# Score matmuls over 512 columns, and expert 0's late rows placed by one-hot matmuls instead of through memory

## The reference

```
# 1: causal linear attention: q,k = relu(.)+1e-6; out = (q k^T masked to s<=t) v / row sum
x = layernorm(x + attn(x) @ out_w.T + out_b)
# 2: cross attention, |t-s| <= 64, keys and values are ctx itself
x = layernorm(x + softmax(q k^T / sqrt(8)) @ ctx @ W_proj + b_proj)
# 3: mixture of 8 experts, top 1, capacity int(4096/8*1.25)+1 = 641 rows each
top1 = argmax(softmax(x @ wg)); rank = tokens of the same expert before this one
slot = top1*capacity + rank           # over capacity: dropped
buf.at[slot].set(x); eb = buf.reshape(8, 641, 128)
y = gelu(eb @ W1 + b1) @ W2 + b2      # hidden width 512
x = layernorm(x + where(valid, y[slot], 0) * score)
```

## Time and profile before

| | us |
|---|---|
| median of 3 runs (463.06 to 465.02) | 464.04 |
| the profiled execution, its own time | 465.73 |
| its span, first to last instruction | 464.0 |
| PE busy in the span | 423.5 |
| DVE, ACT, POOL busy | 346.2, 264.5, 257.7 |

### The profile page before, as it was taken

How to read it: one execution, slowest core, us unless ns; L and a number is a source line. 1 busy time by engine, 2 the same in 40 slices (tenths; PEclk the granted TensorE clock), 3 DMA queues, 4 the chain that set the end, 5 groups by cost and what they waited for, 6 DMA issues and landing times.

```text
span 464.0 us, 21013 instructions
## 1 busy us (share of the span) xinstructions
PE 423.5 (91%) x7874; PEld 336.8 (73%) x7874; DVE 346.2 (75%) x1671; ACT 264.5 (57%) x655; POOL 257.7 (56%) x375
## 2 busy tenths in 40 slices
PE   8889999999999999999999999998857999999950
PEld 6666778787878787878787878776637777777650
DVE  4366667788899898899998899787871667777660
ACT  4455667666777666777666777666551344444400
POOL 5433355665566665566665566554662055566673
PEclk9999999999999999999999999999987999999995
DMA  4800000110011110010110010000016034443100
GB/s 133 277 15 16 14 25 15 32 32 28 26 37 27 31 32 27 26 38 27 33 31 27 26 28 15 14 5 26 26 37 202 8 107 116 114 108 90 31 17 20
DMA packets 25719, 22.50 MB, mean 48 GB/s; under 512 B 3606, under 2 KB 21072, under 8 KB 25620
## 3 DMA queue, kind: packets, MB, share of 16 engines
q1 hardware_dynamic: 23284, 16.96, 12.7%
q0 software_dynamic: 2336, 4.20, 2.9%
HBM read 12.13 MB, written 9.58 MB: 47 GB/s over the span
## 4 chain that ended last, share of the span: by engine, by line
PE 82%; issue 5%; DVE 4%; POOL 3%; ACT 2%; DMA 2%; POOLq 0%; DVEq 0%; ACTq 0%; SPq 0%
PE banks L622 24%; PE banks L678 13%; PE banks L958 9%; PE banks L615 7%; PE banks L630 7%; PE banks L940 6%; PE banks L690 3%; PE banks L706 3%; ACT arena L1160 1%; PE banks L656 1%; PE banks L657 1%; PE banks L658 1%; PE banks L758 1%; PE banks L591 1%; DMA expert_in<-x,sidx 1%
## 5 line engine op out<-in xcount | busy, mean ns | idle before, releaser
L1304 DVE TENSOR_REDUCE mx<-banks 128x8 f32<-128x1024 f32 x64 | 77.9, 1218 | 23.4 <-PE banks L630 23.3
L441 POOL TENSOR_TENSOR rs<-ve,minus_half 128x1 f32<-128x1 f32 x32 | 18.2, 569 | 99.6 <-DVE ve L1271 99.2
L678 PE MATMUL banks<-arena,V 128*32 128x128 f32 x2048 | 69.6, 276 | 0.4 <-ACT arena L1019 0.2
L1019 ACT ACTIVATE arena<-banks 128x1024 f32<-128x1024 f32 x64 | 62.2, 1022 | 10.9 <-PE banks L630 10.9
L1160 ACT ACTIVATE arena<-banks,b1T 128x321 f32<-128x321 f32 x64 | 33.8, 528 | 56.1 <-PE banks L940 55.2
L678 PEld LDWEIGHTS banks<-arena,V 128*32 128x32 f32 x2048 | 52.0, 109 | 10.0 <-issue 5.3
L989 ACT ACTIVATE arena<-banks 64x512 f32<-64x512 f32 x60 | 35.3, 588 | 38.7 <-PE banks L630 38.7
L550 POOL DMA_INDIRECT out_x<-ot,idx x40 | 40.4, 1010 | 20.4 <-DVE ot L1704 11.5
L940 PE MATMUL banks<-arena,w_sb 128*128 128x320 f32 (+1 forms) x128 | 38.5, 442 | 3.4 <-DVE r L1679 2.4
L622 PE MATMUL banks<-QE,kT 32*128 32x128 f32 x1024 | 37.5, 282 | 3.3 <-DVE mx L1304 1.3
L472 POOL DMA_INDIRECT expert_in<-x,sidx x32 | 35.1, 1096 | 9.8 <-issue 6.3
(11 more groups left out here) (176 smaller groups left out, 1021.3 us busy)
## 6 DMA issues: line engine op xcount, KB each, us to landing
w_sb<-in_L_ffn_W SPq DMA_DIRECT2D x16, 256.0 KB
expert_in<-zeros SPq DMA_DIRECT2D x10, 266.5 KB, 3.7
EB<-expert_in SPq DMA_DIRECT2D x8, 325.0 KB
X<-in_x SPq DMA_DIRECT2D x32, 64.0 KB, 2.0
C<-in_ctx SPq DMA_DIRECT2D x32, 64.0 KB, 2.5
out_x<-fb SPq DMA_DIRECT2D x32, 64.0 KB
out_x<-ot,idx POOLq DMA_INDIRECT x40
b2b<-in_L_ffn_b SPq DMA_DIRECT2D x1, 512.0 KB
```

Of the source, the lines that this page charges most:

```text
L678: mm = pe.matmul(bank(name)[VW * s:VW * (s + 1), half * P:(half + 1) * P], V[:, h, :], scored[:, h // NA, h % NA, :], start=q == 0, stop=q ...
L1019: nc.scalar.activation(P2[b % 2][:, 2 * half:2 * half + 2].rearrange("p j a t -> p j (a t)"), pair("s2t", half), ACT.Exp, scale=SCALE).the ...
L1304: v.tensor_reduce(mx[b % 2][:, 8 * half:8 * half + 8].rearrange("p (j a) -> p j a", a=NA), pair("s2", half).rearrange("p j (a t) -> p j a ...
```

## The change

Scores of `s1` and `s2` are now made by `by_slot`: four matmuls (eight in the trace), one for each group of rows, each over the 512 columns of its bank. `s2t` keeps `by_head`, since there the weights differ from slot to slot. After the first four mask matmuls a new semaphore (`s1_half`, `s2_half`, `s2t_half`) is raised, and the first half's reader waits for that.

Expert 0's rows reach PSUM in a new way, for that expert alone. SP loads the weights of experts 0 and 1 in the drain, and the rows of expert 0 as they are after batches 0 to 27 into `EB[2]` (`early_rows`); POOL's scatter of batch 28 waits for that load. PE turns them by matmuls that add into banks 4 and 5. For each of batches 28 to 31 a one-hot matrix (128 tokens by 641 slots) is made, for 28 to 30 by two ACT instructions (square, then relu of 1 minus it) and for 31 by two DVE comparisons, and PE multiplies the batch's rows `x2` by it in two halves (`late_rows`). The 28 filler matmuls are gone. DVE copies the two banks to `ebT`, and the first layer of expert 0 waits for that and no longer for `EB[0]`, which is still loaded for the residual and the gate. Expert 1's rows are turned ahead of the last part of expert 0's second layer. On DVE, rk4 moves up behind rk3 of the same batch.

```diff
+            def early_rows():                      # SP
+                for k in range(4):
+                    sp.wait_ge(scattered[k], 16 * (LATE // 4))
+                sp.dma_start(EB[2][:], buf[0:ET * P, :].rearrange("(p c) d -> p c d", c=ET)).then_inc(early_in, 16)
+                sp.dma_start(ER0[:], buf[ET * P:ROWS, :]).then_inc(early_in, 16)
             for n in range(B + LAST + 1):
                 at(load, n + 4)
+                if n == B - 3:
+                    expert_weights(0)
+                    expert_weights(1)
+                if n == LATE + 7:
+                    early_rows()
...
-            expert_weights(0)
-            expert_weights(1)
...
-            for e in range(1, 3):
-                expert_rows(e)
+            expert_rows(1)
+            sp.wait_ge(early_turned, 1)
+            expert_rows(2)
...
+            g.memset(slot_of[:, ET * P:ROWS], float(ET * P))        # POOL, constants
+            g.iota(slot_of[:, 0:ET * P], pattern=[[1, ET], [ET, P]], base=0, channel_multiplier=0,
+                   allow_small_or_imprecise_dtypes=True).then_inc(slots_ready, 1)
...
+                if b == LATE:                                       # POOL, op_scatter
+                    pool.wait_ge(early_in, 32)
...
+            def by_slot(name, weights, moved):
+                for j, used in enumerate(BANKS[name]):
+                    part = slice(VW * j, VW * (j + 1))
+                    pe.matmul(banks[:, used, :], weights[part, :], moved[part, :, :].rearrange("p a t -> p (a t)"),
+                              start=True, stop=False, tile_position=(VW * j, 0))
...
-                by_head("s1", lambda part, a: kT[b % 2][part, :], lambda part, a: QE[b % 2][part, a, :])
-                causal_masks(0)
+                by_slot("s1", kT[b % 2], QE[b % 2])
+                causal_masks(0).then_inc(s1_half, 1)
                 causal_masks(1).then_inc(s1_full, 1)
...
+            def early_rows():                      # PE
+                pe.wait_ge(early_in, 32)
+                for c in range(ET):
+                    for half, (r0, r1) in enumerate(HALVES):
+                        c0, c1 = max(c * P, r0), min((c + 1) * P, r1)
+                        if c0 < c1:
+                            pe.matmul(max_bank[half][:, c0 - r0:c1 - r0], EB[2][:, c, 0:D], ident[:, c0 - c * P:c1 - c * P],
+                                      start=False, stop=False)
...
+            def late_rows(b, half):
+                if b < B - 1:
+                    pe.wait_ge(hot_ready, b - LATE + 1)
+                else:
+                    pe.wait_ge(hot_last, half + 1)
+                r0, r1 = HALVES[half]
+                mm = pe.matmul(max_bank[half][:, 0:r1 - r0], x2[b % 4][:, 0:D], hot[b - LATE][:, r0:r1],
+                               start=(b == LATE), stop=(b == B - 1))
...
-            for _ in range(WARM):
-                pe.matmul(act_bank[0][:, 0:P], ident[:], ident[:], start=True, stop=True)
...
-                act.wait_ge(s1_full, b + 1)
+                act.wait_ge(s1_full if half else s1_half, b + 1)
...
+            def op_hot(b):                         # ACT, batches 28 to 30
+                to = hot[b - LATE]
+                act.wait_ge(slot_ready, b + 1)
+                nc.scalar.activation(to, slot_of[:], ACT.Square, bias=minus_slot[:, b - LATE:b - LATE + 1]).then_inc(hot_square, 1)
+                act.wait_ge(hot_square, b - LATE + 1)
+                nc.scalar.activation(to, to, ACT.Relu, scale=-1.0, bias=ones[:, 0:1]).then_inc(hot_ready, 1)
...
+            def op_hot(half):                      # DVE, batch 31
+                r0, r1 = HALVES[half]
+                v.tensor_scalar(hot[B - 1 - LATE][:, r0:r1], slot_of[:, r0:r1], slot1[:], None, ALU.is_equal).then_inc(hot_last, 1)
...
+                if e == 0:                         # DVE, rows_turned
+                    for half, (r0, r1) in enumerate(HALVES):
+                        dve.wait_ge(t_full, half + 1)
+                        v.tensor_copy(ebT[0][:, r0:r1], max_bank[half][:, 0:r1 - r0]).then_inc(t_done, 1)
+                    return
```

More of the change, by code:

```diff
@@ L218, in decoder @@
         xg, end = late(end, [ET, D])
+        hot = [hT[1][:, k, :] for k in range(B - LATE)]
         act_bank = [banks[:, k, :] for k in range(4)]
@@ L347, in _ @@
                 load(b)
[L349 to L355, removed]
             def expert_weights(e):
@@ L363, in expert_rows @@
                     eb_in[e % 3], 16)
-            expert_weights(0)
-            expert_weights(1)
+            def early_rows():
[3 more added lines that the diff above has]
+                sp.dma_start(ER0[:], buf[ET * P:ROWS, :]).then_inc(early_in, 16)
+            for n in range(B + LAST + 1):
+                at(load, n + 4)
+                if n == B - 3:
[3 more added lines that the diff above has]
+                    early_rows()
+                if n == 0:
+                    clear_rows()
+                    sp.dma_start(b2b[:], b2.unsqueeze(0).broadcast_to([P, E, D])).then_inc(b2_in, 16)
+                    sp.dma_start(b2r[:], b2).then_inc(b2_in, 16)
+                at(fallback, n - 8)
             for k in range(4):
@@ L810, in _, with claim_rows @@
                 at(op_s1, n)
+            def claim_rows():
+                for used in (4, 5):
+                    pe.wait_ge(*last_on[used])
+            def early_rows():
[6 more added lines that the diff above has]
+                                      start=False, stop=False)
+                pe.matmul(max_bank[1][:, ET * P - HALVES[1][0]:ROWS - HALVES[1][0]], ER0[:, 0:D], ident[0:1, 0:1],
+                          start=False, stop=False).then_inc(early_turned, 1)
+            def late_rows(b, half):
[6 more added lines that the diff above has]
+                               start=(b == LATE), stop=(b == B - 1))
+                if b == B - 1:
+                    mm.then_inc(t_full, 1)
             op_y1T(B - 4)
@@ L903, in _ @@
             op_lg(B - 2)
+            claim_rows()
+            late_rows(B - 4, 0)
             op_rk(B - 3)
+            late_rows(B - 4, 1)
             op_rk(B - 2)
@@ L907, in _ @@
             op_lg(B - 1)
+            early_rows()
             op_rk(B - 1)
+            late_rows(B - 3, 0)
+            late_rows(B - 3, 1)
+            late_rows(B - 2, 0)
+            late_rows(B - 1, 0)
+            late_rows(B - 2, 1)
+            late_rows(B - 1, 1)
             pe.wait_ge(slot_ready, B)
@@ L950, in second_layer @@
                 for k in range(JT):
+                    if e == 0 and k == JT - 1:
+                        turn_rows(1)
                     if e > 0 and k < 2:
@@ L1016, in op_p @@
             def op_p(b, half):
-                act.wait_ge(s2t_full, b + 1)
+                act.wait_ge(s2t_full if half else s2t_half, b + 1)
                 wait(act, pv2_full, b - 1)
@@ L1148, in _ @@
             op_x2Te(B - 1)
+            op_hot(B - 3)
             op_fb(B - 2)
             op_lexp(B - 1)
+            op_hot(B - 2)
             op_fb(B - 1)
@@ L1301, in op_mx @@
             def op_mx(b, half):
-                dve.wait_ge(s2_full, b + 1)
+                dve.wait_ge(s2_full if half else s2_half, b + 1)
                 wait(dve, mxs_ready, b - 1)
@@ L1740, in _ @@
                     break
+                if e == 0:
+                    for c in range(2):
+                        summed(e, c, gate_mark)
+                    rows_turned(1)
                 for c in range(ET):
```

54 lines of the change are left out of this document (37 added, 17 removed).

## The result

The kernel after takes 458.27 us (median of 6 runs, 455.39 to 460.63), the kernel before beside it 463.82 (6 runs, 462.88 to 465.02). The ratio is 0.988, 95% interval 0.984 to 0.992: some 5.6 us, or 1.2%, faster. The forecast was 457.2, which was 6.8 us less than the median of 464.04 it started from. The profiled execution of the kernel after has a time of 458.66 and a span of 456.9, against 465.73 and 464.0.

The account below looks back on a forecast made before the run. PE bounds the kernel (82% of the chain), with one large hole of 10.9 us before expert 0's first layer. 465.73 - 2.0 - 0.3 - 4.5 = 458.9; the median stands 1.7 lower: 457.2 us, range 453.5 to 461.5.

Parts of the forecast that it names:

- Long score matmuls: Loop, `s1` and `s2`: 512-column passes save 0.032 us a group, 2.0 us in 64 groups, with full overlap.
- The rival (475): Loop score groups: long streams overlap less, four groups running only as three at a time, + 16 us; chance 0.05.
- Early signals: Half signals come 0.14 us earlier: worth nothing in the loop, 0.3 us in the filling and the drain.
- In the loop PE waits for nobody, so it is worth nothing there: Loop: the 0.14 us earlier half signal gains 0, as PE's waits show almost nothing, 0.7 us at most.
- the half signals matter in the loop: Rival, loop: PE's `s2` loads begin just when ACT ends its first half; up to 4 us more, 453.3; chance 0.10.
- The drain: After the loop: ranks 31 come 2.2 us late, yet expert 0's first layer starts 6.6 us earlier.
- so I let it rise near 350: Drain: PE's clock rises from 1.2 to 2.4 GHz near 350 us, since fillers saw it rise after 3.5 us.
- the clock stays low: Rival: without fillers expert 0's first layer may run at 1.2 GHz, 4.3 us more at most, 461; chance 0.13.
- The way into expert 1: Expert 0 to expert 1's first layer: 5.2 us earlier, 0.7 lost waiting for banks DVE sums, net 4.5.
- the rival of late rows: Before expert 1: its rows land after 363.7, 3 to 5 us more of scatters and loads, 459 to 461; chance 0.10.
- experts farther apart than 10.1 us: Sign of being wrong, expert phase: experts 1 to 7 starting more than 10.1 us apart.
- The experts follow each other at 10.1 us: Kernel before, after expert 0's first layer: PE is filled again, experts 10.1 us apart.

Follow-up runs that it names:

- e1_long: Kernel before with only the long score matmuls of `s1` and `s2`; 458.02 us, ratio 0.996.
- e2_half: Kernel before with only the early half signals (`s1`, `s2`, `s2t`); 457.01 us, ratio 0.993.
- e5_half_dve: Kernel before with only the half signal of `s2` to DVE's maxima; 459.99 us, one run.
- e6_half_act: Kernel before with only the half signals of `s1` and `s2t` to ACT; 464.14 us, one run.
- e3_loop: Kernel before with long score matmuls and half signals, keeping the old way into expert 0; 455.44 us, ratio 0.990.
- c4_order_fill: Kernel after with ranks 31 ahead of the early rows, ACT reordered to match, and 16 fillers in the drain; 454.44 us, ratio 0.979 to kernel before.
- c3_order: Kernel after with ranks 31 ahead of the early rows and ACT reordered to match, no fillers; 458.67 us, ratio 0.988 to kernel before.
- c6_order_fill_turn: `c4_order_fill` with expert 1's rows turned between expert 0's two layers and copied ahead of expert 0's sums; 451.48 us, ratio 0.972 to kernel before.
- c5_fill_turn: Kernel after with 20 drain fillers, expert 1's rows turned between expert 0's layers and copied ahead of its sums; 453.29 us, ratio 0.975 to kernel before.
- e4_expert: Kernel after with short score matmuls and full signals again, so expert 0's part alone; 458.81 us, ratio 0.997 to kernel before.
- c1_changed: Kernel after, unchanged, run again on another chip; 458.45 us, ratio 0.989 to kernel before.

## Why the forecast came out, point by point

**Long score matmuls: right.** 2.0 forecast, 2.1 measured in `e1_long`; a group shorter by 0.032 us in the forecast and in the trace. The overlap of four row groups is full at 512 columns too. The rival (475) is out by `e1_long`. The Trainium skill (TensorE: Matmul & The Clock Gate, section "Measured speedup vs the span model") has 3.07 times for such four tiles; the trace does not agree: at 0.558 us a round the group would have been 0.23 us longer than before, and it was 0.032 shorter.

**Early signals: the step "In the loop PE waits for nobody, so it is worth nothing there" failed.** It rested on the waits of PE, which have next to nothing of a wait that was put down as "issue"; the row of `s1` in the earlier trace rows, with 3.3 us of idle time, was shown and not used. Measured 3.1 us instead of 0.3 (`e2_half`), through DVE's first maximum of `s2` and not through ACT (`e5_half_dve`, `e6_half_act`). The rival "the half signals matter in the loop" was the case, with 3.1 of its up to 4 us, but the place it named, ACT's half, was not the one, and its time of 453.3 did not come. Both parts of the loop gave 4.7 (`e3_loop`) for 2.3.

**The drain: the step "so I let it rise near 350" failed.** PE was busy 8.00 of 8 us from 344 to 352, and the clock stayed at 1.2 GHz until 352.10, past all but the last microsecond of the rows that I had at 2.4 GHz. The twelve passes of late rows behind ranks 31 took 5.63 us; at 2.4 GHz they take 3.75 in `c4_order_fill`.

The terms, from the loop's end. Up to the ranks of 29 the forecast held: batch 30's logits came 1.15 us late (forecast 1.2), these ranks 1.7 (1.7), batch 31's logits 1.8 (1.6). From those logits to ranks 31, with the early rows between, it took 3.78 us instead of 2.5 (343.90 to 347.68, against 348.5 to 351.0), because all fourteen passes of the early rows ran at the low clock; so ranks 31 came 3.6 late instead of 2.2. From these ranks to the first layer it took 5.54 us instead of 3.5 (351.0 to 354.5). Together the first layer came 3.1 nearer to the loop's end instead of 6.6, and both steps of the miss lie in passes that ran at 1.2 GHz. The DVE comparisons took 0.39 instead of 0.45, its copies 0.49 as forecast. That the clock is the cause, `c4_order_fill` against `c3_order` shows: the same work in the same order with fillers, 4.2 us less at the first layer and in the time.

The rival "the clock stays low" had the kind right and the place wrong: the first layer itself ran at 2.4 GHz, the late and early rows before it did not, although they were "real work of the same density".

One term was mis-sized without harm. ACT's wide instructions, in a timeline of ACT of the kernel after, took 0.83 us instead of 0.70:

```profile
337.98 0.83 ACT L1158 ACTIVATE arena<-slot_of,minus_slot 128x641 f32<-128x641 f32 x1 [1.23 <-DVE x L1463]
```

The 0.85 ns a column of the earlier trace rows was from rows that read PSUM, these read and write SBUF; whether that makes the difference was not tried. The first pair started a little earlier than forecast and ended where the forecast had it, 15.0 us from the loop's end.

**The way into expert 1: right in kind and in size.** The forecast had 1.4 us for the turning at the end of expert 0 with DVE's copies behind it (5.2 of 6.6 kept), and 0.7 lost in the first layer, 2.1 together. Measured: the interval from expert 0 to expert 1 is 11.28 for 10.13, 1.15 more, and expert 1's first layer takes 5.27 for 4.33, 0.94 more, 2.1 together. The latter is the wait for DVE's sums: its second, third and fourth pair of passes each start some 0.15 us behind the end of one. The timeline of PE:

```profile
362.66 0.71 PE L990 MATMUL banks<-ident,EB 128*128 128x128 f32 x5
364.50 5.43 PE L1009 MATMUL banks<-arena,w_sb 128*128 128x321 f32 x16
...
375.48 0.71 PE L1009 MATMUL banks<-arena,w_sb 128*128 128x321 f32 x2
376.50 4.25 PE L1009 MATMUL banks<-arena,w_sb 128*128 128x320 f32 x14 [0.32 <-DVE r L1779]
```

Nearly all of it was avoidable: in `c6_order_fill_turn` the two intervals are 10.35 and 10.03. `EB[1]` was not late, so the slack held; the rival of late rows was out here, and came true in `c5_fill_turn`.

**The sum.** Loop 4.7 for 2.3, expert part 1.3 for 4.5: together 6.0, and the change measured 5.6. Each part was mis-sized by more than the whole was off: the right time came of two wrong terms. The prediction's own sign of being wrong, experts farther apart than 10.1 us, appeared: in the kernel after the starts of experts 1 to 7 lie between 10.2 and 11.0 apart. Of these intervals only the first is put down to the change; in `e4_expert`, on the first chip, all the others are 10.03. "The experts follow each other at 10.1 us" was too short for the kernel before as well, where experts 3 to 7 lie 10.9 to 11.0 apart.

## What to carry to other kernels

Before a wait is called worth nothing, look behind "issue": where an engine writes a bank that another has just read, compare the end of that reader with the start of the writer, since the view of waits can leave it out. The same distance in two kernels, here 0.36 us, says that the writer still waits in both. When gaps are filled with real work, read the granted clock of the stretch and cost all of that work at the level it has there, and do not take from one trace when it will rise; matmuls that keep the clock up before the work is due can be worth more than the work moved. When the profiled execution is not the typical one of its runs, say which of the two a number is from. And an own sequence for the first of many rounds should be measured beside the one that the other rounds have.

## What the runs showed of the hardware

The rhythm of the experts depends on the chip. On the first chip all but the first interval of `e1_long` are 10.03 us. On the others, experts 3 to 7 lie up to 11.0 apart, in the kernel before too. The difference is in DVE's sums. In the kernel after, three of them, and in `e4_expert` (first chip) two:

```profile
372.41 0.35 DVE L1779 SCALAR_TENSOR_TENSOR r<-banks,EB,arena 128x128 f32<-128x128 f32 x1 [0.32 <-PE banks L1029]
373.86 0.35 DVE L1779 SCALAR_TENSOR_TENSOR r<-banks,EB,arena 128x128 f32<-128x128 f32 x1 [0.77 <-PE banks L1029]
376.00 0.35 DVE L1779 SCALAR_TENSOR_TENSOR r<-banks,EB,arena 128x128 f32<-128x128 f32 x1 [1.46 <-PE banks L1029]
```

```profile
377.60 0.35 DVE L1779 SCALAR_TENSOR_TENSOR r<-banks,EB,arena 128x128 f32<-128x128 f32 x1 [0.21 <-PE banks L1029]
378.50 0.35 DVE L1779 SCALAR_TENSOR_TENSOR r<-banks,EB,arena 128x128 f32<-128x128 f32 x1 [0.21 <-PE banks L1029]
```

In the latter they follow PE's parts at 0.9 us; in the former they come 1.5 and 2.1 us apart, and the third starts 2 us after PE has ended its part, and the next expert's first layer waits for their banks. GpSimd's indirect DMAs run in that stretch on both chips. What holds DVE back there was not tried and stays open; it is worth 3.9 us in the distance from expert 0's first layer to expert 7's (74.23 us in the kernel before, 70.31 in `e1_long`), about the difference between the chips' times of the kernel before.

A clock that stays at 1.2 GHz for 8 us in which PE has no gap was not expected: in the kernel before, the fillers had run for 3.5 us when it rose. But that was one trace. In the six traces that have the same 28 fillers they ran between 3.3 and 5.9 us until the clock rose, longest in `e2_half`, where they start at 347.23:

```profile
347.30:353.10 5.80, 5.80 (x27) 5.80 (x28) 0.00 (x0) 1.08 (x1) 1.23 (x2) 0.50 0.71 213
353.20:354.00 0.80, 0.80 (x9) 0.80 (x9) 0.00 (x0) 0.00 (x0) 0.00 (x0) 1.00 0.06 17
```

With the early and late rows PE had run without a gap for 6.5 to 8.3 us when it rose (`e4_expert`, `c1_changed`, the kernel after, `c3_order`). So even the same work does not bring the clock up after the same time, and what makes the rest of the difference these runs do not say.
